# Decoder with a 64-expert last layer: tokens ranked and sent during the second cross attention instead of after it

## What is computed

```python
x = x + _L1_attn_ref(_layernorm(x), ...)
x = x + _L1_xattn_ref(_layernorm(x), ctx_1024, ctx_1024, mask, Wq, Wk, Wv, Wo)
...
# second experts, on xt = _layernorm(x) as 4096 rows of 256
logits = xt @ gate_w.T + gate_b
sel = jnp.argmax(softmax(logits), axis=-1)          # one of 64 experts a token
order = jnp.argsort(sel); xs = xt[order]
counts = jnp.bincount(sel, length=64)
ys = jax.lax.ragged_dot(xs, expert_w, counts)       # 64 weights of 256 x 256
ys = ys + expert_b[sel[order]]
out = zeros.at[order].set(ys)
x = x + out
```

## Time and profile before

| | us |
|---|---|
| median of 3 runs | 2937.98 (2936.36 to 2942.94) |
| span of the profiled execution, first to last instruction | 2938.1 |
| PE busy in it | 2550.3 (87%) |
| DVE busy | 2102.2 (72%) |
| ACT busy | 1429.1 (49%) |
| POOL busy | 992.9 (34%) |

### The profile page before, as it was taken

One profiled execution on the slowest core, in us unless ns is written; L12 is line 12 of the kernel. 1 busy time (PEld: TensorE's weight loads), 2 busy tenths in 40 slices (PEclk: granted clock), 3 DMA queues, 4 the chain that ended last, 5 costly groups with the idle time before them and its releaser, 6 DMA issues. The chain is left out here.

```text
span 2938.1 us, 59757 instructions
## 1 busy us (share of the span) xinstructions
PE 2550.3 (87%) x19892; PEld 2132.9 (73%) x19892; DVE 2102.2 (72%) x4609; ACT 1429.1 (49%) x3356; POOL 992.9 (34%) x1524
## 2 busy tenths in 40 slices
PE   4979699999967899999679999999996979997583
PEld 3857588888866899999668888888885946665231
DVE  5864488988846677777568888888875657774664
ACT  1531143343433677777455556565653547664041
POOL 0000254454510211111155555555533004433266
PEclk8989699999988899999889999999998979998586
DMA  8002000000046755666300000000000743230845
GB/s 304 0 10 107 0 1 1 0 0 0 0 164 237 259 217 216 225 223 221 107 15 14 11 15 7 14 9 13 8 1 28 243 119 86 82 85 13 266 140 168
DMA packets 156637, 266.67 MB, mean 91 GB/s; under 512 B 20944, under 2 KB 130464, under 8 KB 143200
## 3 DMA queue, kind: packets, MB, share of 16 engines
q1 hardware_dynamic: 140400, 215.91, 21.7%
q0 software_dynamic: 11168, 31.21, 3.7%
q10 hardware_dynamic: 4944, 17.96, 1.5%
HBM read 191.85 MB, written 73.17 MB: 90 GB/s over the span
## 5 line engine op out<-in xcount | busy, mean ns | idle before, releaser
L1585 ACT ACTIVATE a_prob<-a_s_ps,a_ntop 128x256 f32<-128x256 f32 x512 | 235.7, 473 | 304.2 <-DVE a_ntop L1670 304.2
L1638 POOL TENSOR_TENSOR a_prob<-a_prob,a_rden 128x1024 f32<-128x1024 f32 x128 | 242.5, 1895 | 302.0 <-DVE a_rden L1675 302.0
L2273 ACT ACTIVATE x1a_prob<-x1a_st_ps,x1a_mask_now 128x512 f32<-128x512 f32 x256 | 162.2, 686 | 93.4 <-PE x1a_st_ps L2192 91.9
L3064 POOL DMA_INDIRECT e0x_xg<-token_rows,e_order x78 | 75.3, 965 | 385.2 <-PE e0x_t_ps L3111 343.0
L1163 ACT ACTIVATE x0b_sq<-x0b_f 128x1024 f32<-128x1024 f32 x64 | 67.9, 1060 | 282.6 <-DVE x0b_f L1237 282.4
L2348 DVE TENSOR_REDUCE x1a_top<-x1a_s_ps 128x4 f32<-128x1024 f32 x128 | 154.9, 1222 | 68.2 <-PE x1a_s_ps L2176 66.4
L1670 DVE TENSOR_REDUCE a_ntop<-a_s_ps 128x4 f32<-128x1024 f32 x128 | 156.2, 1220 | 38.7 <-PE a_s_ps L1508 38.5
L68 PE MATMUL e0x_up_ps<-e0x_xT_high,e0x_up_w_high 128*128 128x256 f32 x624 | 180.4, 289 | 1.1 <-DVE e0x_up_w_low L3188 1.1
L68 PE MATMUL e0x_up_ps<-e0x_xT_high,e0x_up_w_low 128*128 128x256 f32 x624 | 177.6, 285 | 0.0
L68 PE MATMUL e0x_up_ps<-e0x_xT_low,e0x_up_w_high 128*128 128x256 f32 x624 | 177.3, 284 | 0.0
L68 PE MATMUL e0x_y_ps<-e0x_down_w_high,e0x_hT_high 128*128 128x256 f32 x624 | 176.6, 283 | 0.0
(11 more groups left out here) (626 smaller groups left out, 8707.1 us busy)
## 6 DMA issues: line engine op xcount, KB each, us to landing
e0x_up_raw<-up_rows SPq DMA_DIRECT2D x39, 1024.0 KB, 4.9
e0x_down_raw<-down_rows SPq DMA_DIRECT2D x39, 1024.0 KB
x_qk<-head_rows SPq DMA_DIRECT2D x384, 64.0 KB
head_rows<-x1p_rows_out SPq DMA_DIRECT2D x32, 512.0 KB, 3.7
e1w_ew<-in_L_ffn_expert_w_dram SPq DMA_DIRECT2D x8, 2048.0 KB
sorted_tokens<-zeros SPq DMA_DIRECT2D x10, 1024.0 KB, 12.3
sorted_results<-e0x_y SPq DMA_DIRECT2D x39, 256.0 KB
down_rows<-e0w_downT ACTq DMA_DIRECT2D x8, 1024.0 KB, 7.3
```

Source lines behind the costliest of these rows:

```text
L1585: last = act.activation(prob[:, h % RING, n, t, :], s_ps[:, n, t * SEQ:(t + 1) * SEQ], ACT.Exp, bias=ntop[:, h % RING, n, t:t + 1], accum_ ...
L1638: last = pool.tensor_tensor(p, p, scale_of, ALU.mult)
L2273: last = act.activation(prob[:, c % 2, j, 2 * (h % 2):2 * (h % 2) + 2, :], st_ps[:, :, j * SEQ:(j + 1) * SEQ], ACT.Exp, bias=mask_now[:, p ...
```

## The change

1. **Region instead of sorted rows.** The token scratch becomes `expert_tokens` with 32 regions of 4096 rows and 128 empty rows behind them (131,200 rows of 1 KB). Experts e and e + 32 share region e, the first filling it from the front and the second from its end. A token's place depends only on its rank within its expert, so it can be sent before the counts are known.
2. **Clearing.** l0_attention clears only the last 1 MB of the region and the 128 empty rows (9 DMAs of 128 KB). SP gets a program in l1_attention that copies that cleared MB, DRAM to DRAM, over the other 127 MB, and waits for it.
3. **Ranking in the cross attention.** At the end of G's drain DVE adds a one-hot of the batch's tokens and updates running totals (4 instructions). A new piece N (batch offset -4, h = 1, bank 1, between B3 and B0) makes the ranks with two products; DVE drains it with 7 instructions into `gate.places`. At the start of each POOL batch `send` waits for them and issues two indirect DMAs that scatter the normalised tokens, for the batch of four ago. `gn` gets a second buffer. There are five trailing iterations, of which the fourth does the last N and send, and POOL waits for all sends.
4. **Weights.** The expert weights have their final place under buffers of the cross attention and its projection. SP loads 22 of 64 experts at the start of the cross attention, the others when values, query/key and probability buffers are spent.
5. **l1_experts.** `route` and the scatter block are gone. The tile block begins with a plan: counts, needed segments, segment starts, the expert of each segment and the row of each slot (5 small products in turn with some 20 DVE instructions), then `slots` for the way back (three DVE instructions over 128 x 2048). Tiles are gathered from the region by indirect DMAs from POOL; the weights are copied two segments by DVE and two by ACT.
6. **Biases** move into the last block, beside the gathers of results.

```diff
-CLEARS = ROWS // CLEAR_ROWS
+GATES = 64
+REGION = BATCH * SEQ
+REGIONS = GATES // 2
+EMPTY_ROW = REGIONS * REGION
+CLEARED_FIRST = EMPTY_ROW - CLEAR_ROWS
...
@@ l1_attention @@
+            @block.sync
+            def _(sp):
+                block_of = lambda n: scratch.tokens[bass.ds(n * CLEAR_ROWS, CLEAR_ROWS), :].rearrange("(p r) d -> p (r d)", p=P)
+                with sp.Fori(0, CLEARED_FIRST // CLEAR_ROWS) as n:
+                    sp.dma_start(block_of(n), block_of(CLEARED_FIRST // CLEAR_ROWS)).then_inc(s_cleared, 16)
+                sp.wait_ge(s_cleared, 16 * (CLEARED_FIRST // CLEAR_ROWS))
...
@@ l1_cross_attend: order of the pieces, the last entry is the bank @@
+        order = [("M", 1, -1, 0, 0), ("B", 3, -2, 0, 1), ("P", 0, -1, 1, 0), ("N", 0, -4, 1, 1), ("B", 0, -1, 2, 1),
+                 ("P", 1, -1, 3, 0), ("O", 0, -2, 3, 1), ("M", 0, 0, 4, 0), ("B", 1, -1, 4, 1), ("P", 2, -1, 5, 0),
+                 ("R", 0, -3, 5, 1), ("B", 2, -1, 6, 0), ("W", 0, -2, 6, 1), ("P", 3, -1, 7, 0), ("G", 0, -3, 7, 1)]
...
@@ l1_cross_attend, PE @@
+                    elif kind == "N":
+                        pe.wait_ge(s_hot, HOTS * (own + 1))
+                        ranks = bank[:, 0:TPB * gate.EXPERTS]
+                        pe.matmul(ranks, gate.before_r[:], hot[:].rearrange("p t e -> p (t e)"), start=True, stop=False)
+                        last = pe.matmul(ranks, gate.ones_r[:], earlier[:].rearrange("p t e -> p (t e)"), start=False, stop=True)
...
@@ l1_cross_attend, POOL @@
+                    if live(b - 4):
+                        send(b - 4)
...
+                def send(own):
+                    pool.wait_ge(s_place, own + 1)
+                    for t in range(TPB):
+                        tile = TPB * own + t
+                        pool.indirect_dma_start(scratch.tokens, bass.IndirectOffsetOnAxis(ap=gate.places[:, tile:tile + 1], axis=0),
+                                                gn[:, own % 2, t, :], None).then_inc(s_sent[own % 2], 16)
...
@@ l1_cross_attend, DVE @@
+                        dve.tensor_tensor(hot[:], gate.iota_e[:].unsqueeze(1).broadcast_to(shape),
+                                          mine.unsqueeze(2).broadcast_to(shape), ALU.is_equal).then_inc(s_hot, 1)
+                        dve.tensor_scalar(earlier[:, 0, :], gate.total[:], 1.0, None, ALU.mult).then_inc(s_hot, 1)
+                        dve.wait_ge(s_hot, HOTS * own + 2)
+                        dve.tensor_tensor(earlier[:, 1, :], gate.total[:], hot[:, 0, :], ALU.add).then_inc(s_hot, 1)
+                        dve.wait_ge(s_hot, HOTS * own + 3)
+                        dve.tensor_tensor(gate.total[:], earlier[:, 1, :], hot[:, 1, :], ALU.add).then_inc(s_hot, 1)
+                    elif kind == "N":
+                        dve.wait_ge(filled["N"], own + 1)
...
@@ l1_experts, tile block @@
+                @block.gpsimd
+                def _(pool):
+                    pool.wait_ge(s_index, 1)
+                    for i in range(NT):
+                        if i >= D:
+                            pool.wait_ge(s_tp, i - D + 1)
+                        pool.indirect_dma_start(xg[:, i % D, :], None, scratch.tokens,
+                                                bass.IndirectOffsetOnAxis(ap=index[:, i:i + 1], axis=0)).then_inc(s_ld[i % D], 16)
...
@@ l1_experts, last block, DVE @@
+                    dve.tensor_tensor(chosen[:], gate.iota_e[:].unsqueeze(1).broadcast_to([P, TILES, E]),
+                                      gate.found[:].unsqueeze(2).broadcast_to([P, TILES, E]), ALU.is_equal).then_inc(s_chosen, 1)
+                    for t in range(LATE):
+                        add_bias(t)
                     for t in range(TILES):
                         n = t % GATHERS
-                        dve.wait_ge(s_got[n], gathered + 16 * (t // GATHERS + 1))
+                        if t + LATE < TILES:
+                            add_bias(t + LATE)
+                        dve.wait_ge(s_biased, t + 1)
+                        dve.wait_ge(s_got[n], 16 * (t // GATHERS + 1))
                         dve.tensor_tensor(sh.x[:, t, :], sh.x[:, t, :], y[:, n, :], ALU.add).then_inc(s_sum, 1)
```

More of the change, by code:

```diff
@@ L3485, in l1_experts @@
             w_now = sb("w_now", [P, RING, PER, KC, DIM])
+            count, need, start, end = [sb(name, [E, 1]) for name in ("count", "need", "start", "end")]
+            slot_f = sb("slot_f", [P, TILES])
+            room = Room(w_now[:].rearrange("p r g k d -> p (r g k d)"))
+            need_wide = room.take([P])[0:E]
+            started, inside, marked = room.take([PER, NT])[0:E], room.take([PER, NT])[0:E], room.take([PER, 3, NT])[0:E]
+            start_row = room.take([E])
+            within, valid, place, upper, back = [room.take([NT]) for n in range(5)]
@@ new lines, in _ @@
+                    dve.tensor_tensor(valid, within, count_of, ALU.is_lt)
+                    dve.tensor_scalar(upper, expert_of, float(REGIONS), None, ALU.is_ge)
+                    dve.scalar_tensor_tensor(place, expert_of, float(REGION), within, ALU.mult, ALU.add)
+                    step.then(dve.tensor_scalar(back, within, 2.0, FROM_END, ALU.mult, ALU.add))
+                    step.then(dve.tensor_tensor(back, back, upper, ALU.mult))
+                    step.then(dve.tensor_tensor(place, place, back, ALU.subtract))
```

430 lines of the change are left out of this document (265 added, 165 removed).

## The result

The change makes the kernel slower: 2975.52 us median (2967.94 to 2979.28, 4 runs) against 2940.21 (2936.36 to 2942.94, 4 runs), ratio 1.0122, 95% interval 1.0106 to 1.0137. The forecast was 2897.0, and faster. The profiled execution has a span of 2977.4 us, 39.3 more than the one of before.

The account below looks back on a forecast made before the run. PE bounds l1_attention and, with DVE near, the cross attention; a 96.9 us gap without PE's main work was the target. Sum: 2938.1 - 70.1 + 17 + 2 + 0 + 9.9 + 0 = 2897 us, range 2872 to 2945.

Parts of the forecast that it names:

- The gap: Last expert known to first expert product: 96.9 us replaced by 26.8, so 70.1 us less (64 to 74).
- Cross attention, steady batches: Twelve batches lengthen as N waits for B3's drain, the rest of DVE's work hidden: +17 us (10 to 34).
- The drain of the pipeline: End of the cross attention: a send comes between POOL's normalising and its half of the outputs, +2 us (0 to 4).
- Last block: After the tiles: the bias chain at clock 0.50 takes 1.52 us a tile, +9.9 us (0 to +12).
- Clearing: l1_attention: 127 copies of 1 MB stay hidden and gathers land just in time, 0 us (0 to +15).
- the copies delay the gathers: l1_attention: doubled gather latency makes ACT stand 7 us in some 13 batches, PE behind it: +90, 2987 us; chance 0.07.
- copies that outlast the stage: l1_attention: below 180 GB/s the block waits for SP; at 150 GB/s +148, 3045 us; chance 0.13.
- Weights: Cross attention: expert weights issued behind due loads and ahead of the 40 us pipeline emptying, 0 us.
- Tiles: Tile block: 1.54 us a tile as before, 0 us (-5 to +23).
- POOL's gathers: Tile block: gathers slowed beside DVE's copies bound the tiles, 15 us later (2912) or +21 to +23 (2920); chance 0.17.

Follow-up runs that it names:

- spread_weights: Changed kernel with the first 22 expert weights loaded three at a time behind every second batch's loads, not ahead of the first batch: 2959.93 us median, ratio 1.0072.
- n_bank0: Changed kernel with piece N moved behind B0 at h = 2 in bank 0: 2973.99 us median, ratio 1.0096.
- copies_earlier: Changed kernel with the 127 copies moved from l1_attention into the cross attention of layer 0: 2934.7 us median, ratio 0.9986.
- pieces_1k: Changed kernel with the copies kept in l1_attention but made in pieces of one row (1 KB): 2943.14 us median, ratio 1.0002.

## Why the prediction was wrong

**The gap: right.** -67.4 for -70.1. The last send lands at 2808.5, 7.2 us from the last expert for 7.8 forecast, but from there to the plan's first product at 2812.7 it takes 4.2 us where the block change had 1.1: that came from SP's first DMA behind the change, while DVE's first instruction came 2.2 us behind it. The plan took 7.4 for 9.2, the slots 7.2 for 7.6, copies and hand-over 2.7 for 1.1 (DVE and ACT load registers first). That errors of +3.1, +1.6 and -1.8 nearly cancel is in part luck.

**Cross attention, steady batches: right.** With the clock at 1.00 (spread_weights) twelve batches take 15.9 us more than before, 1.3 a batch for 1.4, and PE waits ahead of N as forecast (11.7 us in 12 times). The drain of the pipeline took 1.2 us more for +2. The changed kernel's own profile has 4.3 us more from the clock. That the rest of DVE's added time would be hidden was half wrong (n_bank0), but it moved the sum little.

**Last block: right.** +8.8 for +9.9; the additions of the biases come every 1.50 us for 1.52, at clock 0.50, with PE busy all of the time. What I left out: POOL's gathers took 1.18 us on average beside DVE's two additions a tile for 0.95.

**Clearing: wrong, 0 for +48.8.** The step that failed is the latency. I set the 8.1 us of a gather beside 1 MB loads against the 7.9 us that a batch has the earlier trace rows, wrote "just enough", though 8.1 is already more than 7.9, and took 0. The loads of rows 10 came two at a time with pauses; 127 copies in one queue keep every DMA engine full, and beside their 64 KB packets a gather landed after 12.2 us in the median and 21.6 at most. ACT's 45.7 us came of it and the 26.3 us that PE waited more behind ACT; the other 13.4 of PE's 39.7 are its stall without a visible cause, gone like the rest where the copies stand elsewhere (copies_earlier), and what remains goes with a lower clock. The rate was off too, 325 GB/s for the estimated 209, on the harmless side. The rival "the copies delay the gathers" named the place, the engine that waits and PE behind it, with 7 us a batch; the trace has 45.7 us in 9 times, 5.1 each. It deserved more than 0.07, because its point of decision lay within the accuracy of the two rows. That its 2987 lies near the 2977 of the profile is luck: it had 90 us for this term alone, and 26 of the 80 that came lie in two other stages. The range's end of +15 for this term was short by 34: it had no row behind it. The other rival, copies that outlast the stage, decides at 180 GB/s and was far off.

**Weights: wrong, 0 for +10.8.** I wrote that they are issued behind the loads that are due, which is true of batches 0 and 1, and didn't ask what is queued behind them: batch 2, whose queries and keys PE waits for 26.2 us in place of 14.9. The projection's +2.9 is not assigned: it took 107.9 to 111.0 us in the profiles without a pattern.

**Tiles: wrong, 0 for +15.2.** The sum of DVE was 0.42 + 2 x 0.41 in 1.54 us. It left out that an engine also reads two numbers into registers for each tile, which no busy time shows: DVE's stream took 1.78 us. Before, DVE had 1.5 segments a tile, now 2. The forecast's own rival for this stage, POOL's gathers, gave 2912 and 2920 and thus nearly the right price, +15 to +23, by a mechanism that did not act: POOL waited for PE. That the price is near is luck.

By the Trainium skill's page "SBUF — State Buffer" (Who interferes with whom) a DVE instruction with two SBUF inputs contends with a GpSimd instruction that reads SBUF. A gather reads its index there, and the trace agrees in the gap (3.19 us beside 2.27 us of DVE, 0.99 without it); in the tiles, where gathers and DVE's copies hardly overlap, a gather took 0.97 us on average.

The range (2872 to 2945) would have had to take all three delays nearly in full; each was judged hidden by its own row, and the errors were all on the same side. Without the three, 2977.4 - 48.8 - 10.8 - 15.2 = 2902.6, the forecast's case.

## What to carry to other kernels

A transfer that is "free" because its stage has idle DMA engines is only free if nobody there waits for a small DMA: set the latency of a small DMA beside such traffic (here 12.2 us beside packets of 64 KB, 6.7 beside 1 KB, 2.8 alone) against the slack of that DMA (here 7.9), and put bulk traffic where there is no gather. Take the length of a packet from those that carry the bytes and not from a mean over all. For a moved load ask what is queued behind it, not only what it stands behind. When engines trade work in a loop whose addresses are read at run time, count the register loads: about 0.65 us of DVE's instruction stream for each value here, and busy time shows none of it.

## What was not expected of the hardware

- Copies from DRAM to DRAM ran at 321 to 330 GB/s on average in packets of 64 KB and of 1 KB alike (pieces_1k 321, the changed kernel 325, copies_earlier 330). The Trainium skill's page "DMA: Bandwidth & Descriptors" (Latency and other measured facts) gives 207 to 214 GB/s for copies between HBM tensors, measured with rows of 16 KB that lie 512 KB or more apart; this case's trace, with contiguous blocks of 1 MB, doesn't show that rate.
- One load instruction for two registers took 0.53 us, two for one register 0.30 each.
- The granted clock of a PE-bound stage without any differing line varied between 0.92 and 1.00 from profile to profile, up to 20 us of the kernel's time, more than several of the edits. Stage marks and the clock beside them were needed to read an edit at all.
